# First attention: DVE's reciprocal and product of a chunk move behind the next chunk's first row maxima

## The chip, the cores and the metric

One core of a Trainium2 chip runs the whole program. The metric is the device time of one execution in microseconds (us). PE is TensorE, DVE is VectorE, ACT is ScalarE, POOL is GpSimd, SP is SyncE.

## The reference, cut to what matters

The program is an attention layer with clipped relative positions over 4096 tokens of width 256 (16 heads of 16), a layernorm, a two-layer local attention block and another layernorm. The change touches the first attention alone:

```python
qh, kh, vh = split(q @ in_proj_weight.T + in_proj_bias)      # 16 heads, d = 16
qh = qh / sqrt(d)
scores = einsum('bhid,bhjd->bhij', qh, kh)
bias_r = einsum('bhid,rd->bhir', qh, rel_pe)                 # 129 distances, clipped at 64
attn = softmax(scores + take_along_axis(bias_r, rel), axis=-1)
out = einsum('bhij,bhjd->bhid', attn, vh)
```

## The kernel before, in words

`attend` works through 128 chunks: 16 heads by 8 blocks of 512 queries, numbered n. Scores are exact to float32 by way of bfloat16 parts. For each chunk PE makes the scores twice. The first time, 32 products of 128 queries by 512 keys (`max_group`, L490) go one at a time into a bank of `shared_ps`, and DVE takes the maximum of every row of it (`bank_max`, L764 and 765). The second time, with keys in the rows (`score`, L516 and 519) and the row maxima subtracted in the same product, they go to `scores`, DVE adds the bias near the diagonal (`near_add`, L738 and 741), ACT takes the exponential of two tiles at a time (`exp_pair`, L639 to 642), and PE multiplies with the values (`pv_quad`, L531). PE puts four key tiles of one turn in four quarters of its array, so `out_ps` holds four partial sums. At the end of a chunk ACT copies `out_ps` to `out_copy` (L665), PE turns it with four transposes (`sum_quadrants`, L551), and DVE's `finish` adds the quarters (L773), takes the reciprocal of the softmax sum (L775) and multiplies (L777) into `attn`, which the trace calls tokens.

The engines are ordered by hand with semaphores. PE goes through a chunk in 8 turns: one value product, then four slots, each a max product for a later chunk (slot s of chunk n makes product 16 + s; from slot 16 on it is chunk n + 2's), and two or none of the score products of two turns further on. In turns 0 and 1 of chunks 0 to 118 half of the bias block nine further on comes last (`make_bias`, L542, 16 small products), which ACT moves to SBUF (L633). DVE goes through the same 32 slots: the maximum of each, with a near add or the finding and cutting of the row maxima (`find_max` L748, `cut_high` L755, `cut_low` L759) before or after some, and `finish` behind the last.

Three banks `shared_ps` go round among 36 uses in a fixed order, `SHARED_USES`: maxima 0 to 3, bias half 0, maxima 4 to 7, bias half 1, maxima 8 to 19, rows, maxima 20 to 31, sum. Before each use PE's `bank_free` (L460 to 475) waits for the reader of the use three places before. So slot 3 waits for the maximum of slot 0, the first bias half for the maximum of slot 1, slot 4 for that of slot 2, and slot 2 for the sum of the chunk before: by `normed`, which the product at L777 raises.

DVE, PE and ACT run pairs of chunks (even, odd) in loops; DVE's is `Fori(0, 63)` at L804 with the last two chunks written out behind it. I call the seam between an even and the next odd chunk inner, and the seam where a DVE loop goes round, from an odd to an even chunk, turning.

Of the kernel before, what the change touches and what calls it, by code (L numbers as in the profile page):

```python
# [19 lines left out]
ALU = mybir.AluOpType  # L20
AX = mybir.AxisListType
# [10 lines left out]
D = E // HEADS  # L32
# [13 lines left out]
VW = D + 1  # L46
# [187 lines left out]
def attend(nc, q_parts, k_parts, v_wide, rel_T, ident, attn):  # L234
# [10 lines left out]
    TOTAL = HEADS * CHUNKS  # L245
# [4 lines left out]
    with ExitStack() as ctx:  # L250
        sb = lambda name, shape, dt=F32: ctx.enter_context(nc.sbuf_tensor(name, shape, dt))
        ps = lambda name, shape, dt=F32: ctx.enter_context(nc.psum_tensor(name, shape, dt))
        sem = lambda name: ctx.enter_context(nc.semaphore(name))
# [22 lines left out]
        out_sum = sb("out_sum", [P, TPC, VW])  # L276
# [4 lines left out]
        inv_sum = sb("inv_sum", [P, TPC, 1])  # L281
# [31 lines left out]
        max_rows = sem("max_rows")  # L313
# [4 lines left out]
        pv_done = sem("pv_done")  # L318
        out_copied = sem("out_copied")
        out_summed = sem("out_summed")  # L320
        norm_step = sem("norm_step")
        normed = sem("normed")

        block = ctx.enter_context(nc.Block())
# [1 line left out]
        def place(n):  # L326

            return n // CHUNKS, n % CHUNKS
# [131 lines left out]
        def _(pe):  # L460
            def bank_free(n, bias, *use):

                at = SHARED_USES.index(use) - 3
                if not bias and at >= 0 and SHARED_USES[at][0] == "bias":
                    at -= 3
                m = n if at >= 0 else n - 1
                kind, i = SHARED_USES[at]
                if kind == "max":
                    pe.wait_ge(max_read, m * MAX_GROUPS + (MAX_GROUPS + LEAD + i + 3))
                elif kind == "bias":  # L470
                    pe.wait_ge(bias_read, (m + NEXT_GEN) * 2 + (i + 1))
                elif kind == "rows":
                    pe.wait_ge(max_placed, m + 2)
                else:
                    pe.wait_ge(normed, m + 2)

            def max_group(n, par, k, bank):

# [88 lines left out]
            def chunk(n, par, bias, ahead):  # L567


                for turn in range(QUADS):  # L570
                    pv_quad(n, par, turn)
                    for i in range(4):
                        slot = 4 * turn + i
                        if slot == ROWS_SLOT and ahead:
                            if ahead == 2:
                                bank_free(n, bias, "rows", 0)
                            max_to_rows(n + 1, 1 - par)
                        max_slot(n, par, bias, slot, ahead)
                        for c in SLOT_SCORES[i]:
                            if turn < QUADS - 2:  # L580
                                score(n, par, 4 * (turn + 2) + c)
                            elif ahead:
                                score(n + 1, 1 - par, 4 * (turn - QUADS + 2) + c)
                    if bias and turn < 2:
                        bank_free(n, bias, "bias", turn)
                        make_bias(n + NEXT_GEN, (par + NEXT_GEN) % 2, turn)
                if ahead == 2:
                    bank_free(n, bias, "sum", 0)
                else:
                    pe.wait_ge(max_placed, TOTAL)  # L590
                    pe.wait_ge(normed, n + 1)
                sum_quadrants(n, par)

            pe.wait_ge(consts_in, 32)
# [28 lines left out]
        @block.scalar  # L623
        def _(act):
            act.preload_act_table(ACT.Exp)
            act.sem_inc(exp_done, 2)
            for semaphore in (out_copied, normed, out_summed, max_rows):
                act.sem_inc(semaphore, 1)

            def keep_bias(block_no, half):  # L630
                h, b = place(block_no)
                act.wait_ge(bias_ready, block_no * 2 + half + 1)
                act.activation(near_bias[:, bass.ds(h % 2, 1), 1:TILES + 1, bass.ds(b * BLOCK_U + half * UG, UG)],  # L633
                               shared("bias", half).rearrange("p (a u j) -> p a j u", a=1, u=UG), ACT.Copy
                               ).then_inc(bias_read, 1)

            def exp_pair(n, s):
                if s in (0, 1, 2, PAIRS - 1):
                    act.wait_ge(near_added, n * 4 + {0: 1, 1: 2, 2: 3, PAIRS - 1: 4}[s])  # L639
                act.wait_ge(scores_ready, n * PAIRS + s + 1)  # L640
                act.wait_ge(pv_done, n * QUADS + s // 2 + 1)
                act.activation(probs[s % 4][:], scores[s % 2][:], ACT.Exp).then_inc(exp_done, 1)  # L642

            def place_max(n, par):
                act.wait_ge(max_rows, n + 2)
                act.activation(queries[par][ROWS:ROWS + MROWS, :], shared("rows", 0)[ROWS:ROWS + MROWS, :], ACT.Copy
                               ).then_inc(max_placed, 1)

            def chunk(n, par, bias, more):

                for s in range(4, PAIRS):
                    if s == PAIRS - 2 and more:
                        place_max(n + 1, 1 - par)
                    exp_pair(n, s)
                    if bias and s in (5, 7):
                        if s == 5:
                            act.wait_ge(window_ready, n + 1)
                        keep_bias(n + NEXT_GEN, s // 7)
                for s in range(4):
                    if more:  # L660
                        exp_pair(n + 1, s)
                    if s == 1:
                        act.wait_ge(pv_done, n * QUADS + QUADS + 2)
                        act.wait_ge(out_summed, n + 1)
                        act.activation(out_copy[:], out_ps[:], ACT.Copy).then_inc(out_copied, 1)  # L665

            act.wait_ge(cleared, 10)
            for e in range(NEXT_GEN):
                for half in range(2):
                    keep_bias(e, half)  # L670
            place_max(0, 0)
            for s in range(4):
                exp_pair(0, s)
            last_bias = (TOTAL - NEXT_GEN) // 2
            with act.Fori(0, last_bias) as m:
                for par in range(2):
                    chunk(m * 2 + par, par, True, True)
            chunk(2 * last_bias, 0, True, True)
            chunk(2 * last_bias + 1, 1, False, True)
            with act.Fori(last_bias + 1, TOTAL // 2 - 1) as m:  # L680
                for par in range(2):
                    chunk(m * 2 + par, par, False, True)
            chunk(TOTAL - 2, 0, False, True)
            chunk(TOTAL - 1, 1, False, False)

        @block.vector
        def _(dve):
# [77 lines left out]
                dve.tensor_reduce(group_max[par][:, k:k + 1], bank, AX.X, ALU.max  # L765
                                  ).then_inc(max_read, 1)

            def finish(n):
                h, c = place(n)
                dve.wait_ge(out_summed, n + 2)  # L770
                dve.wait_ge(normed, n + 1)
                quarters = shared("sum", 0).rearrange("p (t i e) -> p t e i", i=4, e=P // 4)
                dve.tensor_reduce(out_sum[:], quarters[:, :, 0:VW, :], AX.X, ALU.add).then_inc(norm_step, 1)  # L773
                dve.wait_ge(norm_step, n * 2 + 1)
                dve.reciprocal(inv_sum[:], out_sum[:, :, D:VW]).then_inc(norm_step, 1)  # L775
                dve.wait_ge(norm_step, n * 2 + 2)
                dve.tensor_tensor(attn[:, bass.ds(c * TPC, TPC), bass.ds(h * D, D)], out_sum[:, :, 0:D],  # L777
                                  inv_sum[:].to_broadcast([P, TPC, D]), ALU.mult).then_inc(normed, 1)

            def chunk(n, par, ahead):  # L780
                for slot in range(MAX_GROUPS):
                    k = LEAD + slot
                    if slot == NEAR_SLOTS[3]:
                        near_add(n, PAIRS - 1)
                    if ahead and slot in NEAR_SLOTS[:3]:
                        near_add(n + 1, NEAR_SLOTS.index(slot))
                    if k < MAX_GROUPS and ahead >= 1:
                        bank_max(n + 1, 1 - par, k, shared("max", slot))
                    if k >= MAX_GROUPS and ahead >= 2:
                        bank_max(n + 2, par, k - MAX_GROUPS, shared("max", slot))  # L790
                    if ahead >= 1 and MAX_GROUPS - 1 <= k <= MAX_GROUPS + 1:
                        (find_max, cut_high, cut_low)[k - MAX_GROUPS + 1](n + 1, 1 - par)
                finish(n)

            for k in range(MAX_GROUPS):
                bank_max(0, 0, k, shared_ps[k % 3][:])
# [4 lines left out]
                bank_max(1, 1, k, shared_ps[(MAX_GROUPS + k) % 3][:])  # L801
            for s in range(3):
                near_add(0, s)
            with dve.Fori(0, TOTAL // 2 - 1) as m:  # L804
                for par in range(2):
                    chunk(m * 2 + par, par, 2)
            chunk(TOTAL - 2, 0, 1)
            chunk(TOTAL - 1, 1, 0)


def layernorm_params(dve, pool, stats, mean, rstd, scratch, expo, step, first):
# [1025 lines left out]
```

## Time and profile before

| | us |
|---|---|
| median of 3 runs | 5559.55 |
| lowest, highest | 5557.49, 5559.81 |
| the profiled execution's own time | 5559.1 |
| its span | 5557.4 |
| PE busy in the span | 5118.3 (92%) |
| DVE busy | 4185.6 (75%) |
| ACT busy | 3111.0 (56%) |
| first and last quarter sum (L773) | 285.7, 3752.4 |

The quarter sum ends each of the 128 chunks, so the stage lasts some 3470 us of the span, and two neighbouring quarter sums mark one chunk's period. PE's matmuls are pipelined: a product of 512 columns is shown with 0.38 us, while the next starts 0.22 us after it. Busy shares therefore say less than the starts do.

### The profile page before, as it was taken

What the parts mean: (1) busy time and instruction counts of PE and PEld (TensorE: products, weight loads), DVE (VectorE), ACT (ScalarE), POOL (GpSimd) and SP (SyncE); (2) the same over time, 40 slices, a digit from 0 to 9 for tenths busy, and PEclk for the clock granted to TensorE, in tenths of its full rate; (3) what the DMA queues carried; (4) which work ended last, traced back from release to release, by engine and by line L of the source; (5) the groups of instructions that cost most, each with busy time, mean ns of one, the idle gap of its engine ahead of it and who ended that gap; (6) DMA issues with size and microseconds to landing.
All of it is one profiled execution on the core that took longest, in us unless ns stands there. A gap on an engine that the chain in (4) does not pass through costs nothing. (4 is left out here: it accounts for less than half of the span.)

```text
span 5557.4 us, 114988 instructions
## 1 busy us (share of the span) xinstructions
PE 5118.3 (92%) x33760; PEld 2655.6 (48%) x33760; DVE 4185.6 (75%) x8817; ACT 3111.0 (56%) x4539; POOL 997.1 (18%) x791
## 2 busy tenths in 40 slices
PE   7599999999999999999999999998599989899989
PEld 4233333333333333333333333334488867788866
DVE  6488888888888888888888888871477744677755
ACT  4266666666666666666666666670266532456521
POOL 0211111111111111111111111100233310233211
PEclk9599999999999999999999999995699999999999
DMA  6312212212122122121221211211200000000010
GB/s 203 76 49 55 54 48 54 52 52 54 49 55 54 48 54 54 49 54 48 54 54 48 55 48 48 52 40 33 95 1 0 0 17 0 17 0 0 1 38 23
DMA packets 199610, 248.32 MB, mean 45 GB/s; under 512 B 60575, under 2 KB 128485, under 8 KB 197733
## 3 DMA queue, kind: packets, MB, share of 16 engines
q1 hardware_dynamic: 194388, 226.76, 14.9%
q0 software_dynamic: 5136, 20.45, 1.9%
q8 instruction: 50, 0.82, 0.1%
q14 instruction: 36, 0.29, 0.0%
HBM read 210.72 MB, written 36.18 MB: 44 GB/s over the span
## 5 line engine op out<-in xcount | busy, mean ns | idle before, releaser
L765 DVE TENSOR_REDUCE group_max<-shared_ps 128x1 f32<-128x512 f32 x4096 | 2668.6, 686 | 536.6 <-PE shared_ps L490 430.6
L642 ACT ACTIVATE probs<-scores 128x1024 f32<-128x1024 f32 x2048 | 2012.0, 1021 | 995.7 <-PE scores L516 619.4
L490 PE MATMUL shared_ps<-keys,max_queries 96*128 96x512 bf16 x4096 | 1444.0, 385 | 10.8 <-issue 1.7
L516 PE MATMUL scores<-queries,keys 98*128 98x512 bf16 (+3 forms) x4096 | 1212.8, 370 | 92.6 <-ACT probs L642 91.5
L531 PE MATMUL out_ps<-probs,values 128*17 128x512 f32 x8192 | 1079.1, 599 | 0.4 <-ACT probs L642 0.4
L490 PEld LDWEIGHTS shared_ps<-keys,max_queries 96*128 96x128 bf16 x4096 | 395.2, 96 | 1149.2 <-DVE group_max L765 544.2
L231 POOL TENSOR_TENSOR near_window<-near_bias,one_f 128x1536 bf16<-128x1536 f32 x128 | 351.4, 2746 | 2909.1 <-DVE max_parts L759 2263.7
L516 PEld LDWEIGHTS scores<-queries,keys 98*128 98x128 bf16 x4096 | 359.0, 98 | 466.2 <-ACT probs L642 242.8
L542 PE MATMUL shared_ps<-block_q,block_table 96*128 96x32 bf16 x4096 | 271.6, 233 | 107.6 <-POOL block_q L427 80.7
L542 PEld LDWEIGHTS shared_ps<-block_q,block_table 96*128 96x128 bf16 x4096 | 231.3, 114 | 197.9 <-issue 148.6
L1191 POOL TENSOR_TENSOR norm<-norm,layer_expo 128x16 f32<-128x16 f32 x64 | 186.2, 2910 | 705.4 <-DVE norm L1577 705.4
L1449 ACT ACTIVATE sim_prob<-sim_prob,shift,norm 128x256 f32<-128x256 f32 x512 | 299.5, 588 | 10.0 <-DVE shift L1647 10.0
L531 PEld LDWEIGHTS out_ps<-probs,values 128*17 128x17 f32 x8192 | 136.1, 95 | 264.7 <-issue 191.4
L494 PE MATMUL shared_ps<-ident_b,near_window 128*128 128x128 bf16 x1536 | 255.4, 220 | 0.0
L633 ACT ACTIVATE near_bias<-shared_ps 128x512 f32 (+1 forms) x256 | 152.8, 597 | 179.5 <-PE shared_ps L542 179.4
L741 DVE TENSOR_TENSOR scores<-scores,near_bias 128x192 f32<-128x192 f32 (+2 forms) x768 | 234.2, 334 | 20.7 <-PE scores L516 16.5
L1297 PEld LDWEIGHTS bank<-v_kept,prob_T 128*128 128x128 f32 x2048 | 238.2, 192 | 7.5 <-issue 2.0
L1297 PE MATMUL bank<-v_kept,prob_T 128*128 128x64 f32 x2048 | 235.8, 274 | 1.2 <-DVE tokens L1609 1.2
L1429 ACT ACTIVATE squares<-bank 128x512 f32<-128x512 f32 x128 | 76.5, 598 | 262.5 <-PE bank L1250 262.5
L494 PEld LDWEIGHTS shared_ps<-ident_b,near_window 128*128 128x128 bf16 x1536 | 151.3, 99 | 123.3 <-issue 2.2
L1504 ACT ACTIVATE gate<-quad,b 128x512 f32<-128x512 f32 x96 | 66.1, 688 | 236.9 <-PE quad L1371 236.9
L1642 DVE CUSTOM_DVE_ANT_0 sim_prob<-quad,mask 128x256 f32<-128x256 f32 x512 | 181.9, 420 | 16.5 <-issue 13.3
(195 smaller groups left out, 5777.3 us busy)
## 6 DMA issues: line engine op xcount, KB each, us to landing
keys<-k_parts SPq DMA_DIRECT2D x384, 96.0 KB, 2.1
values<-v_wide SPq DMA_DIRECT2D x128, 272.0 KB, 2.7
keys<-k_parts SPq DMA_DIRECT2D x384, 64.0 KB, 2.0
keys<-k_parts SPq DMA_DIRECT2D x128, 132.0 KB, 2.4
k_parts<-part SPq DMA_DIRECT2D x96, 128.0 KB
queries<-q_parts SPq DMA_DIRECT2D x768, 16.0 KB, 1.7
max_queries<-q_parts SPq DMA_DIRECT2D x768, 16.0 KB, 1.7
keys<-k_parts SPq DMA_DIRECT2D x384, 32.0 KB, 1.9
```

The source lines that it names most:

```text
L231: return pool.tensor_tensor(out, in_, ones[:].to_broadcast(list(in_.shape)), ALU.mult)
L490: mm = pe.matmul(bank, max_queries[par][:, t * P:(t + 1) * P], keys[par][0:ROWS, (t + TPC * g) * P:(t + TPC * (g + 1)) * P], start=True, s ...
L494: mm = pe.matmul(bank[:, pos * P:(pos + 1) * P], near_window[par][:, slab, u:u + P], ident_b[:], start=False, stop=i == len(near) - 1)
L516: mm = pe.matmul(out[:, 0:cut], keys[par][:, c * P:(c + 1) * P], queries[par][:, 0:cut], start=True, stop=True)
L531: mm = pe.matmul(out_ps[32 * i:32 * i + VW, :], values[par][:, 4 * q + i, :], probs[(2 * q + i // 2) % 4][:, i % 2, :], start=q == 0, stop ...
L542: mm = pe.matmul(shared("bias", half)[:, i * TILES:(i + 1) * TILES], block_table[par][:, BLOCK_U - 1 - u:BLOCK_U - 1 - u + P], block_q[par ...
L642: act.activation(probs[s % 4][:], scores[s % 2][:], ACT.Exp).then_inc(exp_done, 1)
L741: ins = dve.tensor_tensor(part, part, near_bias[:, bass.ds(h % 2, 1), bass.ds(c * TPC + slab, 1), u:u + b - a], ALU.add)
L765: dve.tensor_reduce(group_max[par][:, k:k + 1], bank, AX.X, ALU.max).then_inc(max_read, 1)
L1191: pool.tensor_tensor(norm[par][:], norm[par][:], expo[:, 0:2 * LHEADS].rearrange("p (h a) -> p h a", a=1), ALU.pow).then_inc(S.norm_ready, 1)
L1297: mm = pe.matmul(o_ps[:, j * LD:(j + 1) * LD], prob_T[:, 2 * j + c, :], v[:, h * LD:(h + 1) * LD], start=c == 0, stop=c == 1)
L1449: ins = act.activation(prob[:, h, :], sim[:, h, :], ACT.Exp, bias=shift[:, head:head + 1], scale=norm[par][:, head, :], accum_out=total[:, ...
```

## The change

`finish` is cut in three. `add_quarters` (the sum) stays at the end of the chunk and raises `sum_read`; on this PE now waits for the sum bank, in place of `normed`. `invert` (the reciprocal) of chunk n stands in chunk n + 1 behind the maximum of slot 0, and `finish` (the product) behind the maximum of slot 1. The first two chunks are taken out of DVE's loop, which starts at 1, since chunk 0 has none before it; the last chunk's reciprocal and product stand behind the last chunk. The semaphore `norm_step` becomes `sum_read` and `inverted`.

```diff
--- before.py
+++ after.py
@@ -318,7 +318,8 @@
         pv_done = sem("pv_done")
         out_copied = sem("out_copied")
         out_summed = sem("out_summed")
-        norm_step = sem("norm_step")
+        sum_read = sem("sum_read")
+        inverted = sem("inverted")
         normed = sem("normed")
 
         block = ctx.enter_context(nc.Block())
@@ -472,7 +473,7 @@
                 elif kind == "rows":
                     pe.wait_ge(max_placed, m + 2)
                 else:
-                    pe.wait_ge(normed, m + 2)
+                    pe.wait_ge(sum_read, m + 2)
 
             def max_group(n, par, k, bank):
 
@@ -588,7 +589,7 @@
                     bank_free(n, bias, "sum", 0)
                 else:
                     pe.wait_ge(max_placed, TOTAL)
-                    pe.wait_ge(normed, n + 1)
+                    pe.wait_ge(sum_read, n + 1)
                 sum_quadrants(n, par)
 
             pe.wait_ge(consts_in, 32)
@@ -624,7 +625,7 @@
         def _(act):
             act.preload_act_table(ACT.Exp)
             act.sem_inc(exp_done, 2)
-            for semaphore in (out_copied, normed, out_summed, max_rows):
+            for semaphore in (out_copied, sum_read, normed, out_summed, max_rows):
                 act.sem_inc(semaphore, 1)
 
             def keep_bias(block_no, half):
@@ -765,21 +766,27 @@
                 dve.tensor_reduce(group_max[par][:, k:k + 1], bank, AX.X, ALU.max
                                   ).then_inc(max_read, 1)
 
-            def finish(n):
-                h, c = place(n)
+            def add_quarters(n):
                 dve.wait_ge(out_summed, n + 2)
                 dve.wait_ge(normed, n + 1)
                 quarters = shared("sum", 0).rearrange("p (t i e) -> p t e i", i=4, e=P // 4)
-                dve.tensor_reduce(out_sum[:], quarters[:, :, 0:VW, :], AX.X, ALU.add).then_inc(norm_step, 1)
-                dve.wait_ge(norm_step, n * 2 + 1)
-                dve.reciprocal(inv_sum[:], out_sum[:, :, D:VW]).then_inc(norm_step, 1)
-                dve.wait_ge(norm_step, n * 2 + 2)
+                dve.tensor_reduce(out_sum[:], quarters[:, :, 0:VW, :], AX.X, ALU.add).then_inc(sum_read, 1)
+
+            def invert(n):
+                dve.wait_ge(sum_read, n + 2)
+                dve.reciprocal(inv_sum[:], out_sum[:, :, D:VW]).then_inc(inverted, 1)
+
+            def finish(n):
+                h, c = place(n)
+                dve.wait_ge(inverted, n + 1)
                 dve.tensor_tensor(attn[:, bass.ds(c * TPC, TPC), bass.ds(h * D, D)], out_sum[:, :, 0:D],
                                   inv_sum[:].to_broadcast([P, TPC, D]), ALU.mult).then_inc(normed, 1)
 
-            def chunk(n, par, ahead):
+            def chunk(n, par, ahead, before):
                 for slot in range(MAX_GROUPS):
                     k = LEAD + slot
+                    if before and slot in (1, 2):
+                        (invert, finish)[slot - 1](n - 1)
                     if slot == NEAR_SLOTS[3]:
                         near_add(n, PAIRS - 1)
                     if ahead and slot in NEAR_SLOTS[:3]:
@@ -790,7 +797,7 @@
                         bank_max(n + 2, par, k - MAX_GROUPS, shared("max", slot))
                     if ahead >= 1 and MAX_GROUPS - 1 <= k <= MAX_GROUPS + 1:
                         (find_max, cut_high, cut_low)[k - MAX_GROUPS + 1](n + 1, 1 - par)
-                finish(n)
+                add_quarters(n)
 
             for k in range(MAX_GROUPS):
                 bank_max(0, 0, k, shared_ps[k % 3][:])
@@ -801,11 +808,15 @@
                 bank_max(1, 1, k, shared_ps[(MAX_GROUPS + k) % 3][:])
             for s in range(3):
                 near_add(0, s)
-            with dve.Fori(0, TOTAL // 2 - 1) as m:
+            for n in range(2):
+                chunk(n, n, 2, n > 0)
+            with dve.Fori(1, TOTAL // 2 - 1) as m:
                 for par in range(2):
-                    chunk(m * 2 + par, par, 2)
-            chunk(TOTAL - 2, 0, 1)
-            chunk(TOTAL - 1, 1, 0)
+                    chunk(m * 2 + par, par, 2, True)
+            chunk(TOTAL - 2, 0, 1, True)
+            chunk(TOTAL - 1, 1, 0, True)
+            invert(TOTAL - 1)
+            finish(TOTAL - 1)
 
 
 def layernorm_params(dve, pool, stats, mean, rstd, scratch, expo, step, first):
```

## Rows read from the trace of the kernel before

**Rows 1.** Busy us (instructions) of PE, PEld, DVE, ACT, POOL; PE clock; DMA; attention stage.

```profile
1500.00:2500.00 1000.00, 963.46 (x6653) 366.44 (x6651) 838.75 (x1593) 652.87 (x726) 163.08 (x138) 1.00 0.21 52
```

**Rows 2.** Waits of PE's weight loads, 286 to 3300 us: total, times, longest.

```profile
PEld shared_ps L490 <- DVE group_max L765: 448.8, 583, 0.9
```

**Rows 3.** Order of time, DVE, inner seam: start, duration, line, tiles, count.

```profile
1938.89 1.29 DVE L765 TENSOR_REDUCE group_max<-shared_ps 128x1 f32<-128x512 f32 x2 [0.18 <-PE shared_ps L490]
1940.09 0.43 DVE L773 TENSOR_REDUCE out_sum<-shared_ps 128x68 f32<-128x272 f32 x1
1940.56 0.18 DVE L775 RECIPROCAL inv_sum<-out_sum 128x4 f32<-128x4 f32 x1
1940.95 0.22 DVE L777 TENSOR_TENSOR tokens<-out_sum,inv_sum 128x64 f32 x1 [0.21 <-DVE inv_sum L775]
1941.09 0.68 DVE L765 TENSOR_REDUCE group_max<-shared_ps 128x1 f32<-128x512 f32 x1
...
1941.69 1.28 DVE L765 TENSOR_REDUCE group_max<-shared_ps 128x1 f32<-128x512 f32 x2
```

**Rows 4.** Order of time, PE, inner seam.

```profile
1938.47 0.60 PE L490 MATMUL shared_ps<-keys,max_queries 96*128 96x512 bf16 x2
...
1940.42 0.39 PE L490 MATMUL shared_ps<-keys,max_queries 96*128 96x512 bf16 x1
...
1941.08 0.38 PE L490 MATMUL shared_ps<-keys,max_queries 96*128 96x512 bf16 x1
...
1941.73 0.60 PE L490 MATMUL shared_ps<-keys,max_queries 96*128 96x512 bf16 x2
1942.50 0.50 PE L542 MATMUL shared_ps<-block_q,block_table 96*128 96x32 bf16 x6 [0.17 <-DVE group_max L765]
...
1944.49 0.39 PE L490 MATMUL shared_ps<-keys,max_queries 96*128 96x512 bf16 x1
```

**Rows 5.** Order of time, DVE, turning seam.

```profile
1967.49 0.43 DVE L773 TENSOR_REDUCE out_sum<-shared_ps 128x68 f32<-128x272 f32 x1
...
1968.35 0.23 DVE L777 TENSOR_TENSOR tokens<-out_sum,inv_sum 128x64 f32 x1 [0.21 <-DVE inv_sum L775]
...
1968.91 1.89 DVE L765 TENSOR_REDUCE group_max<-shared_ps 128x1 f32<-128x512 f32 x3 [0.33 <-PE shared_ps L490]
```

**Rows 6.** Order of time, PE, turning seam.

```profile
1967.82 0.39 PE L490 MATMUL shared_ps<-keys,max_queries 96*128 96x512 bf16 x1
...
1969.65 0.39 PE L490 MATMUL shared_ps<-keys,max_queries 96*128 96x512 bf16 x1
1970.33 0.90 PE L542 MATMUL shared_ps<-block_q,block_table 96*128 96x32 bf16 x13 [0.28 <-DVE group_max L765]
```

**Rows 7.** DVE's sequencer, ns: the loop's end, the product's registers.

```profile
L804 DVEq COMPARE_BRANCH  x63: 50/56/72, 314.5 to 3716.2; - x63
...
L777 DVEq FUSED_REGOPS  x126: 129/129/129, 286.4 to 3715.9; - x126
```

**Rows 8.** Order of time, DVE: the quarter sum one chunk later.

```profile
1995.22 0.43 DVE L773 TENSOR_REDUCE out_sum<-shared_ps 128x68 f32<-128x272 f32 x1
```

**Rows 9.** The same behind chunks without bias: inner, turning, inner seam.

```profile
3589.13 0.43 DVE L773 TENSOR_REDUCE out_sum<-shared_ps 128x68 f32<-128x272 f32 x1
...
3614.24 0.43 DVE L773 TENSOR_REDUCE out_sum<-shared_ps 128x68 f32<-128x272 f32 x1
...
3639.62 0.43 DVE L773 TENSOR_REDUCE out_sum<-shared_ps 128x68 f32<-128x272 f32 x1
```

**Rows 10.** Order of time, DVE: small operations between row maxima.

```profile
1955.34 0.16 DVE L755 TENSOR_SCALAR max_parts<-row_max 128x4 bf16<-128x4 f32 x1
1955.50 0.69 DVE L765 TENSOR_REDUCE group_max<-shared_ps 128x1 f32<-128x512 f32 x1
1956.11 0.15 DVE L759 SCALAR_TENSOR_TENSOR max_parts<-row_max,max_parts 128x4 bf16<-128x4 f32 x1
1956.26 1.29 DVE L765 TENSOR_REDUCE group_max<-shared_ps 128x1 f32<-128x512 f32 x2
```

## The prediction

> **What bounds the kernel now.** I read the table of engines over the attention stage first [rows 1]. From 1500 to 2500 us PE is busy for 963 us at full clock, DVE for 839, ACT for 653: the stage goes at PE's pace, with small holes, so a change on DVE is worth only what it takes out of PE's holes. Next the list of waits of PE and of its weight loads. At its head stand PE's max products, waiting for DVE's row maxima (L765) [rows 2]; the product of line 777, whose `normed` the sum bank waits for, is nowhere in it. Many of those idle times of PEld lie under running value products and cost nothing, so the seam between two chunks has to be read instruction by instruction.
>
> Two seams follow each other in time. DVE's loop holds two chunks. After the even one (the inner seam) DVE just goes on; after the odd one (the turning seam) it goes round its loop. Take DVE's quarter sum (L773) as zero: 1940.09 at the inner seam [rows 3], 1967.49 at the turning one [rows 5]. Up to there both are alike: reciprocal at +0.47, product at +0.86. Then the first row maximum starts at +1.00 (1941.09) at the inner seam, and at +1.42 (1968.91) at the turning seam, where the sequencer does the loop's end in between [rows 7]. On PE [rows 4, 6] slot 0's max product starts at +0.33 at both, slot 1's at +0.99. Slots 2 and 3 start at +1.64 and 0.22 us later at the inner seam (two products in 0.60 us, one alone 0.38); at the turning seam slot 3 slips to 1969.65, +2.16, just after the end of slot 0's maximum (1968.91 + 0.68). The half block of bias (L542) takes the bank of slot 1's maximum. That maximum starts 0.60 behind the first and ends at 1941.69 + 0.68 = 1942.37 (+2.28), and the bias starts at 1942.50 (+2.41), 0.13 us later; at the turning seam the same steps give 1968.91 + 0.60 + 0.68 = 1970.19, and the bias starts at 1970.33 (+2.84). PE could have begun it 0.22 us after slot 3, near +2.08. Each seam has a hole ahead of the bias: 0.33 us inner, 0.75 us turning.
>
> Does the hole reach the period? Between quarter sums lie 27.40 us behind an inner seam and 27.73 us behind a turning one [rows 3, 5, 8]: of 0.42 us more lateness 0.33 us arrives. Without bias halves (last chunks) it is 25.11 against 25.38 [rows 9].
>
> **The change part by part.**
>
> *The bank is given back by the sum instead of the product.* The bank comes free at +0.43 instead of +1.09 (0.86 + 0.23 us). Its next user is slot 2's product on PE at +1.64, with no idle time ahead of it [rows 4]. The cover is 0.55 us; worth 0.
>
> *Reciprocal and product leave the place ahead of the first maximum.* Slot 0's product starts at +0.33 and takes 0.39 [rows 3, 4, 6]; a maximum that waits for its product starts 0.04 after that model end (+0.33 + 0.39 + 0.04 = +0.76; the 0.04 as at 1938.47 + 0.38 against 1938.89 in [rows 3, 4]). The sum ends at +0.43, so DVE is free. The loop's end stood behind the product; now it stands behind the sum. From the product's start to the maximum's it took 0.56 us (1968.35 to 1968.91), so from the sum's start +0.56, before +0.76, even if the sequencer were no further ahead. Its 63 turns are thus covered by the wait for PE. Slot 0's maximum: +0.76 to +1.44 at both.
>
> *Reciprocal between the maxima of slots 0 and 1.* The trace has no reciprocal there, but it has two operations of the same size between maxima: `cut_high` and `cut_low`, 0.16 and 0.15 us, each with a wait on DVE's own semaphore, start 0.61 after a maximum's start and put the next one off by 0.16 [rows 10]. The bounds: 0.15 from below (`cut_low`) and, from above, all overlap lost, as rival 3 works out. I take the nearest, 0.16: reciprocal +1.36, maximum of slot 1 +1.52 (its product is there at 0.99 + 0.43 = +1.42), end +2.20, bias at +2.33. That is 0.08 earlier than now at the inner seam, 0.50 at the turning one (0.51 by rounding).
>
> *Product between slots 1 and 2.* It starts at +2.12, and its register work (0.13 us [rows 7]) fits under the running maximum. Maxima of slots 2 and 3 then start near +2.30 and +2.90, against +2.20 and +2.80 at the inner seam. Their banks are wanted by slots 4 and 5, and slot 4 runs at 1944.49, +4.40 [rows 4], 1.3 us after the maximum of slot 2 would end: worth 0. The four own-semaphore waits per chunk stay four. The two peeled chunks add code once, no work; the last chunk's reciprocal and product end the stage as before, worth 0.
>
> *What is late next.* Behind the bias PE runs the turns without a hole of this kind; the exponentials and near adds near the chunk's end follow PE's scores, and they moved with it at the turning seam. They keep 0.09 of 0.42.
>
> **Sum.** Chunks 1 to 118 make bias and lie behind a seam each: 59 of each kind. The 63 turns of DVE's loop leave four turning seams without bias [rows 7]. Turning: 0.33 (as measured between the kinds) + 0.08; inner: 0.08. 59 x 0.49 = 28.9 us. The four without bias: 25.38 - 25.11, 4 x 0.27 = 1.1 us. Together 30.0 us. The profiled execution took 5559.1 us (span 5557.4 and 1.7 around it); 5559.1 - 30.0 = 5529.1. The median of the runs is 0.45 above that execution: 5529.5 us. What a measurement can tell here is about 0.2%, 11.1 us.
>
> By the Trainium skill ("VectorE: DVE Perf Modes", The DRAIN you can't avoid) the next operation doesn't start until the pipe is empty, semaphores cost nothing extra, and what counts is the number of operations. By that alone the move would give PE the bank of slot 1 later, not earlier; rival 3 works out this mechanism from rows. The rows speak against it as an absolute rule: a maximum of 0.68 us is followed by the next 0.60 after its start [rows 3].
>
> **The rivals.**
> 1. *Only the loop's turn is cured.* The reciprocal costs 0.24 and not 0.16, so the inner seam gains nothing and the turning one exactly the measured 0.33: 59 x 0.33 + 1.1 = 20.6 us, 5539 us. For it: no reciprocal was seen in that place. Against: `cut_high` and `cut_low` [rows 10]. Chance 0.15.
> 2. *Everything passes.* The 0.09 us that got lost between lateness and period belong to the even chunk's code and not to a slack: 59 x (0.50 + 0.08) + 1.1 = 35.3 us, 5524 us. Chance 0.13.
> 3. *Slower: the reciprocal stands in front of the bias bank.* Place: between maxima 0 and 1 at all 118 seams. If each operation waits for the end of the one before and the sequencer prepares the next maximum's wait only then, the reciprocal starts at +1.48, ends +1.66, and slot 1's maximum comes 0.33 later (the idle time before a maximum at the turn [rows 5]): +1.99, end +2.67, bias +2.80. Inner +0.39, turning -0.03: 59 x 0.36 - 1.1 = 20 us slower, 5579 us; with the 0.21 us that the product waited behind the reciprocal [rows 3] instead, bias +2.68: 5567 us. It loses from a maximum of slot 1 later than about +1.77. For it: that 0.21 us. Against: that idle time was a true dependence plus register work, and slot 1 does not depend on the reciprocal. Chance 0.06, some of it within 0.2%.
> 4. *Nothing arrives.* PE is earlier at the bias and stands longer for the exponentials at the chunk's end, or the branch isn't hidden: within 3 us of 5559 us. Against: the two kinds of chunk show 0.33 of 0.42 arriving. Chance 0.08.
>
> The change can fail to do what it says only in its first half, and there I expect it: the earlier release is not what pays.
>
> **How the numbers follow.** Forecast 0.58. The range reaches from just past rival 2 (5524, with 4 us for what the later stages make of another start) to past rival 1 (5539, with 7 us for a mixture with rival 4): 5520 to 5546 us. Left out are rivals 3 and 4 and strays, under 2 in 10. Faster by over 0.2%: forecast, rivals 1 and 2, 0.86; within: rival 4 and a little of 3, 0.09; slower 0.05.
>
> **What would show it.** Right: the first maximum at +0.76 from the sum at both seams, reciprocal +1.36, slot 1's maximum +1.52, product +2.12, bias near +2.33 at both; slot 3 never at +2.16; periods near 27.3 us behind both seams. Wrong: a first maximum at the turn later than +0.8 (branch not hidden); over 0.2 us between reciprocal and slot 1's maximum (rivals 1, 3); bias at +2.33 but periods above 27.4 (rival 4); an idle time of PE on line 773 (the bank did matter).

## The result, and the profile after

| | before | after |
|---|---|---|
| median, us | 5559.68 (4 runs) | 5515.00 (4 runs) |
| span of the profiled execution | 5557.4 | 5512.2 |
| first to last quarter sum | 285.7 to 3752.4 | 287.4 to 3709.2 |
| period behind an inner seam | 27.40 | 27.21 |
| period behind a turning seam | 27.73 | 27.17 |

The ratio is 0.9919, with a 95% interval of 0.9902 to 0.9936: 44.7 us faster, where 30.0 were forecast, and below the range's lower end of 5520. Between the first and the last quarter sum lie 3421.8 us instead of 3466.7, so 44.9 us come from the attention stage. The first sum comes 1.7 us later and the rest of the program takes 2.0 us less. That rest has no edit in it; in the kernels below it took between 1803 and 1807 us, so I read nothing into it. In the experiments the kernel before ran again beside each: 5561.63 us (median of 18) with experiments 1 to 4, 5560.72 (one) with 5, 5560.80 (median of 7) with 6 and 7; their ratios are to these.

DVE at the inner seam after the change, in order of time (start, duration, line, tiles, count). It answers to [rows 3].

```profile
1919.45 0.43 DVE L773 TENSOR_REDUCE out_sum<-shared_ps 128x68 f32<-128x272 f32 x1
1920.20 0.69 DVE L766 TENSOR_REDUCE group_max<-shared_ps 128x1 f32<-128x512 f32 x1 [0.32 <-PE shared_ps L491]
1920.81 0.17 DVE L777 RECIPROCAL inv_sum<-out_sum 128x4 f32<-128x4 f32 x1
1920.90 0.66 DVE L766 TENSOR_REDUCE group_max<-shared_ps 128x1 f32<-128x512 f32 x1
1921.47 0.22 DVE L782 TENSOR_TENSOR tokens<-out_sum,inv_sum 128x64 f32 x1
```

PE at the same seam, answering to [rows 4].

```profile
1919.78 0.39 PE L491 MATMUL shared_ps<-keys,max_queries 96*128 96x512 bf16 x1
...
1920.44 0.38 PE L491 MATMUL shared_ps<-keys,max_queries 96*128 96x512 bf16 x1
...
1921.09 0.60 PE L491 MATMUL shared_ps<-keys,max_queries 96*128 96x512 bf16 x2
1921.69 1.07 PE L543 MATMUL shared_ps<-block_q,block_table 96*128 96x32 bf16 x16
```

With the sum as zero, the first maximum starts at +0.75, the reciprocal at +1.36, slot 1's maximum at +1.45, the product at +2.02, slots 2 and 3 of PE at +1.64 and 0.22 later, the bias half at +2.24. The turning seam, from the same two views, no longer differs ([rows 5, 6]; its sum is at 1946.66, and the bias half starts at +2.23):

```profile
1946.66 0.43 DVE L773 TENSOR_REDUCE out_sum<-shared_ps 128x68 f32<-128x272 f32 x1
1947.41 0.69 DVE L766 TENSOR_REDUCE group_max<-shared_ps 128x1 f32<-128x512 f32 x1 [0.32 <-PE shared_ps L491]
```

```profile
1948.30 0.60 PE L491 MATMUL shared_ps<-keys,max_queries 96*128 96x512 bf16 x2
1948.89 0.50 PE L543 MATMUL shared_ps<-block_q,block_table 96*128 96x32 bf16 x6
```

The next quarter sum is at 1973.83. So the bias half starts 0.17 us earlier at inner seams and 0.61 at turning ones, and the periods are 0.19 and 0.56 us shorter in these rows. Over the middle of the stage two chunks take 54.39 us instead of 55.13: 0.74 us a pair, 59 x 0.74 = 43.7 us.

### The profile page after: what moved, and what is told of

It is laid out like the page before. It is cut to its first block and busy times, and to the rows that moved or that the text cites. A ratio compares the mean times of both kernels' runs of the same rounds, so it can differ in the third digit from the quotient of the medians.

```text
span 5512.2 us, 114702 instructions
## 1 busy us (share of the span) xinstructions
PE 5105.0 (93%) x33760; PEld 2653.6 (48%) x33760; DVE 4166.2 (76%) x8817; ACT 3112.3 (56%) x4539; POOL 997.2 (18%) x791
```

## The experiments

Theory A throughout: at the seam PE waits with the bias half for slot 1's maximum, and whatever moves that maximum moves the period. The rivals stand with each run. Positions are counted from the quarter sum.

**1. The release alone.** The kernel before, with `sum_read` raised by the sum and PE waiting for it (the same wait stands a second time for the last chunks):

```diff
-                    pe.wait_ge(normed, m + 2)
+                    pe.wait_ge(sum_read, m + 2)
...
-                dve.tensor_reduce(out_sum[:], quarters[:, :, 0:VW, :], AX.X, ALU.add).then_inc(norm_step, 1)
+                dve.tensor_reduce(out_sum[:], quarters[:, :, 0:VW, :], AX.X, ALU.add).then_inc(sum_read, 1)
```

> The kernel before with one edit: PE's waits for the sum bank go to a semaphore that the quarter sum raises (sum_read) and no longer to the product's. Reciprocal and product stay where they were. Theory A (what counts is when the maximum of slot 1 ends, because the bias half waits for its bank): nothing moves, bias at +2.41 and +2.84 from the quarter sum, periods 27.4 and 27.7 us, 5560 us within 4. Rival B (the 15 us beyond the forecast come from the earlier release of the sum bank): periods shorter by 0.1 us, about 5545 us.

Measured: 5559.68 us, ratio to the kernel before 0.9996 (0.9986 to 1.0006). Bias at +2.41 and +2.84, periods 27.38 and 27.73. Alone, the first half of the change is worth nothing; rival B is out.

**2. The order alone.** The changed kernel, with PE waiting for the product again:

```diff
-                    pe.wait_ge(sum_read, m + 2)
+                    pe.wait_ge(normed, m + 2)
```

> The changed kernel with one edit: PE waits for the sum bank until the product has ended (normed), as before the change. Reciprocal and product stay behind the first maxima. Theory A: the product ends at +2.24, so slot 2's product on PE starts at +2.30 and not at +1.64, slot 3 at +2.52, the bias at +2.74: 0.33 us later than before the change at inner seams, 0.10 earlier at turning ones, and some 0.5 us per seam without bias: 59 x 0.23 + 4 = 18 us slower than before, about 5577 us. Rival C (the order alone brings the gain, the release is idle in every arrangement): 5515 us.

Measured: 5580.39 us, ratio 1.0030 (1.0018 to 1.0041): slower than the kernel before. PE in order of time at an inner seam (sum at 1948.82); the bracket is the idle time and who ended it:

```profile
1950.03 0.60 PE L517 MATMUL scores<-queries,keys 98*128 98x512 bf16 x2
1951.12 0.61 PE L491 MATMUL shared_ps<-keys,max_queries 96*128 96x512 bf16 x2 [0.49 <-DVE tokens L782]
1951.56 0.62 PE L543 MATMUL shared_ps<-block_q,block_table 96*128 96x32 bf16 x8
```

Slot 2 at +2.30 and bias at +2.74, as worked out. The release is idle while the product stands at +0.86 and is worth 65 us (5580 against 5515) once the product stands at +2.02. Rival C is out: the release alone is worth nothing, the order alone costs some 20 us, and together they bring 45.

**3. Only the loop's end out of the way.** The changed kernel with both operations at the start of the next chunk:

```diff
-                    if before and slot in (1, 2):
-                        (invert, finish)[slot - 1](n - 1)
+                    if before and slot == 0:
+                        invert(n - 1)
+                        finish(n - 1)
```

> The changed kernel with reciprocal and product moved to the very start of the next chunk, ahead of slot 0's maximum: the order of DVE's work is that of before, but the loop's end stands ahead of them. Theory A: reciprocal at +0.47, product at +0.86, first maximum at +1.00 at both seams, bias at +2.41 at both, periods 27.41 and 27.37: 59 x 0.35 + 1 = 22 us faster than before, 5538 us. So half of the change's 45 us is the loop's end. Rival D (the loop's end costs nothing of its own, it is only seen in the place where DVE stands idle): 5560 us.

Measured: 5545.9 us, ratio 0.9969 (0.9957 to 0.9982); 8 us above theory A's number. The inner seam is as expected (bias +2.41, period 27.39). At the turning seam DVE's rows, in order of time, show why:

```profile
1962.73 0.43 DVE L773 TENSOR_REDUCE out_sum<-shared_ps 128x68 f32<-128x272 f32 x1
1963.19 0.18 DVE L777 RECIPROCAL inv_sum<-out_sum 128x4 f32<-128x4 f32 x1
1963.76 0.22 DVE L782 TENSOR_TENSOR tokens<-out_sum,inv_sum 128x64 f32 x1 [0.38 <-DVE inv_sum L777]
1963.90 1.28 DVE L766 TENSOR_REDUCE group_max<-shared_ps 128x1 f32<-128x512 f32 x2
```

The product comes at +1.03 and not +0.86, behind an idle time of 0.38 us in place of the 0.21 of [rows 3]. The loop's end is hidden (no gap but this one), but the product's address now has the chunk before this turn's in it, and the view of its line shows 186 blocks of register work for 124 products, up to 206 ns long, where [rows 7] had one of 129 ns each:

```profile
L782 DVEq FUSED_REGOPS  x186: 62/129/206, 316.1 to 3678.9; - x186
```

So bias at +2.58 and period 27.52 at this seam: of the 0.42 us of the loop's end, 0.17 came back as register work. In the changed kernel the same work lies under slot 1's maximum and costs nothing. Expectation missed in this term, theory A kept; rival D is out by the 15 us gained.

**4. Half the turns.** The kernel before, DVE's loop with four chunks in its body:

```diff
-            with dve.Fori(0, TOTAL // 2 - 1) as m:
-                for par in range(2):
-                    chunk(m * 2 + par, par, 2)
+            with dve.Fori(0, TOTAL // 4 - 1) as m:
+                for step in range(4):
+                    chunk(m * 4 + step, step % 2, 2)
+            for step in range(2):
+                chunk(TOTAL - 4 + step, step, 2)
```

> The kernel before with DVE's loop of four chunks instead of two: 31 turns, not 63, nothing else moved. Theory A: 30 turning seams with bias and 2 without become inner ones, at 0.31 to 0.43 us and 0.27 us each: 10 to 13 us faster, 5547 to 5550 us; the periods behind the removed turns fall from 27.72 to 27.4 us and those behind the remaining ones stay. Rival D (the loop's end costs nothing): 5560 us.

Measured: 5729.84 us, ratio 1.0311 (1.0288 to 1.0334). Nobody expected that. DVE in order of time at a removed turn with the sum that follows it, and at a turn that is left with the sum that follows it:

```profile
2057.06 0.43 DVE L773 TENSOR_REDUCE out_sum<-shared_ps 128x68 f32<-128x272 f32 x1
...
2084.37 0.43 DVE L773 TENSOR_REDUCE out_sum<-shared_ps 128x68 f32<-128x272 f32 x1
...
2111.75 0.43 DVE L773 TENSOR_REDUCE out_sum<-shared_ps 128x68 f32<-128x272 f32 x1
...
2112.61 0.23 DVE L777 TENSOR_TENSOR tokens<-out_sum,inv_sum 128x64 f32 x1 [0.21 <-DVE inv_sum L775]
2115.82 0.69 DVE L765 TENSOR_REDUCE group_max<-shared_ps 128x1 f32<-128x512 f32 x1 [2.99 <-issue]
...
2144.43 0.43 DVE L773 TENSOR_REDUCE out_sum<-shared_ps 128x68 f32<-128x272 f32 x1
```

At the turn DVE stands 2.99 us for nothing that the profile names, and the period behind it is 32.68 us, 5.37 more than behind a removed turn (27.31). The idle time is only the first part of this. Slot 3's product waits for slot 0's maximum, so PE stands as well, and then its granted clock falls to half. PE in order of time, and the engines from 2116.37 to 2123.20 us (the last three numbers are PE's clock, the share of the DMA engines and GB/s):

```profile
2116.57 0.61 PE L490 MATMUL shared_ps<-keys,max_queries 96*128 96x512 bf16 x1 [2.80 <-DVE group_max L765]
```

```profile
2116.37:2123.20 6.83, 6.56 (x33) 2.36 (x34) 3.32 (x6) 1.96 (x3) 0.00 (x0) 0.50 0.00 0
```

PE stands for 2.80 us without a product. Near the end of that, at 2116.37, it is given half its clock, 1.2 GHz of 2.4, for 6.83 us, and the same product is shown with 0.61 us and not with 0.38. The first maximum comes 3.07 us later than behind a removed turn (+4.07, not +1.00); the other 2.3 us of the 5.37 I put down to this stretch at half clock. No run has the stall without the fall, so this split is not tested. Before it, and from 2123.20 to the chunk's end, the clock is full. So here the period grows by more than the lateness, the expectation that periods behind the remaining turns stay was missed, and theory A needs the condition that PE's clock stays where it was; over the attention stage of the kernel before and of the changed one the granted clock is 1.00.

The queues of the page have one line that changed much, the instruction queue q14, first of this kernel and then of the kernel before:

```profile
q14 instruction: 187, 1.53, 0.1%
```

```profile
q14 instruction: 36, 0.29, 0.0%
```

151 packets of instructions more for 31 turns, nearly five a turn, 1.2 MB in all. The Trainium skill ("Runtime: NRT & Kernel Launch", Instruction fetch mechanics) says that an engine holds a window of two blocks of instructions, that prefetch is sequential and that a taken branch out of the window has to fetch first; the packets and the 2.99 us agree with it, and the body of two chunks (0.33 us idle in [rows 5], few packets) seems to lie within it. I did not try a body of three. What this run was made for it shows all the same: behind the removed turn the period is 2084.37 - 2057.06 = 27.31 us against 27.73 [rows 5, 8]. All of the 0.42 us arrives. The expected gain of 10 to 13 us can't be seen in the time, since the turns that are left cost far more than it.

**5. A dose of lateness.** The changed kernel with two, then five more reciprocals behind the first:

```diff
+                for i in range(2):
+                    dve.reciprocal(spare[:, :, i:i + 1], out_sum[:, :, D:VW])
```

> The changed kernel with two more reciprocals of the same 128x4 into a spare tile right behind the first, between the maxima of slots 0 and 1. Theory A (a lateness of slot 1's maximum reaches the period in full): they put the maximum off by some 0.2 to 0.3 us in all, the bias by as much, and the periods behind both seams grow by the same amount, 118 times it: 5539 to 5551 us. Rival F (a quarter is absorbed at the chunk's end, as my sum had it): the periods grow by three quarters of the shift of the bias.

> The same with five more reciprocals. Theory A: the shift of the bias is two and a half times that with two more, and the periods follow it one to one: about 5575 to 5605 us. Rival F: three quarters of it.

DVE in order of time with two more (sum at 1928.32), and PE's bias half; the table below has medians over the stage's seams, so a single row can be 0.01 us off:

```profile
1929.68 0.17 DVE L778 RECIPROCAL inv_sum<-out_sum 128x4 f32<-128x4 f32 x1
1929.76 0.22 DVE L780 RECIPROCAL spare<-out_sum 128x4 f32<-128x4 f32 x2
1929.89 0.66 DVE L767 TENSOR_REDUCE group_max<-shared_ps 128x1 f32<-128x512 f32 x1
```

```profile
1930.68 0.50 PE L544 MATMUL shared_ps<-block_q,block_table 96*128 96x32 bf16 x6
```

| | bias half, inner and turning | period behind inner, turning | pair | one run (changed kernel: median of 4), us |
|---|---|---|---|---|
| changed kernel | +2.24, +2.24 | 27.21, 27.18 | 54.39 | 5515.0 |
| two more | +2.37, +2.37 | 27.34, 27.35 | 54.69 | 5533.6 |
| five more | +2.57, +2.56 | 27.54, 27.46 | 55.00 | 5553.7 |

The bias moves by 0.26 and 0.65 us a pair, the pair's period by 0.30 and 0.61: one to one within 0.04. Rival F (three quarters) would give 0.20 and 0.49. The other traces say the same of a pair, by medians: the change moves the bias by -0.77 us and the period by -0.74, experiment 2 by +0.24 and +0.27, experiment 3 by -0.25 and -0.22. The price was wrong again in the same direction: a reciprocal behind another puts the maximum off by 0.065 us, not by 0.1 or more, so both times stayed under theory A's ranges. By the time alone three quarters of the time that theory A adds (5533 to 5542 us with two more) would have fitted the first run; it is the periods, set against the bias in the same trace, that rule F out.

**6. Nothing between the first four maxima.** The reciprocal ahead of slot 4 and the product ahead of slot 5; and the reciprocal ahead of slot 0, the product ahead of slot 4:

```diff
-                    if before and slot in (1, 2):
+                    if before and slot in (4, 5):
```

> The changed kernel with the reciprocal ahead of slot 4's maximum and the product ahead of slot 5's, so that nothing stands between the first four maxima. Theory A: slot 1's maximum starts when its product is there, +1.41 instead of +1.45, bias at +2.21; periods shorter by 0.03 us, 3 us in all, about 5512 us. Rival E (the reciprocal between the maxima is what still holds the bias up): 0.09 us a seam, 5505 us.

```diff
+                    if before and slot in (0, 4):
```

> The changed kernel with the reciprocal ahead of slot 0's maximum, behind the loop's end, and the product ahead of slot 4's. Theory A: the reciprocal lies in the time in which DVE waits for slot 0's product (+0.43 to +0.75) and costs nothing: first maximum +0.75, second +1.41, bias +2.21, about 5512 us as with both later. Rival D' (a reciprocal ahead of the first maximum costs its 0.18 us or more): first maximum +0.9 or later, bias past +2.3, over 5522 us.

Measured, one run each: 5525.3 and 5515.6 us. In both, slot 1's maximum starts at +1.41 and the bias half at +2.23: without any reciprocal in the way it comes 0.01 us earlier. The reciprocal in its present place costs 0.04 us at the maximum and nearly nothing at PE, so rival E is out; and ahead of slot 0 it lies in the wait for PE, so D' is out. Theory A's gain of 3 us did not show either. With both later, periods are 0.07 us longer than the changed kernel's. The difference sits in turn 1: the second bias half waits for the bank of slot 5's maximum, and the product now stands ahead of that one. First DVE, then PE at that place (sum at 1923.03); in the changed kernel this half starts at +6.05, here at +6.13, and in the second order, with the product ahead of slot 4, at +6.04:

```profile
1928.29 0.21 DVE L782 TENSOR_TENSOR tokens<-out_sum,inv_sum 128x64 f32 x1
1928.42 1.28 DVE L766 TENSOR_REDUCE group_max<-shared_ps 128x1 f32<-128x512 f32 x2
```

```profile
1929.16 0.67 PE L543 MATMUL shared_ps<-block_q,block_table 96*128 96x32 bf16 x9
```

**7. The bias half one slot earlier.** If the wait of the bias half is the hole, another order on PE closes it. Made on the changed kernel and on the kernel before:

```diff
-        SHARED_USES = (max_uses[:4] + [("bias", 0)] + max_uses[4:8] + [("bias", 1)]
-                       + max_uses[8:ROWS_SLOT] + [("rows", 0)] + max_uses[ROWS_SLOT:] + [("sum", 0)])
+        SHARED_USES = (max_uses[:3] + [("bias", 0)] + max_uses[3:7] + [("bias", 1)]
+                       + max_uses[7:ROWS_SLOT] + [("rows", 0)] + max_uses[ROWS_SLOT:] + [("sum", 0)])
...
-                    if bias and turn < 2:
+                        if bias and turn < 2 and i == 2:
```

> The changed kernel with one edit on PE: in turns 0 and 1 of a chunk the half block of bias comes ahead of the fourth slot and not behind it, and has its place so in the order of the three banks. It then waits for the maximum of slot 0 (end +1.44) and not of slot 1 (+2.11). Theory A (the wait of the bias half for slot 1's bank was the last hole at the seam): bias at +1.87, slot 3 near +2.87, turn 1's value product 0.16 us earlier than at present at each of 118 seams; chunks without bias lose 0.25 us each, since slot 3 now waits for slot 1. 118 x 0.16 - 8 x 0.25 = 17 us under the changed kernel, about 5498 us. Rival G (the next limit, ACT's or DVE's work in the turn, stands right behind): 5512 us or more.

> The kernel before with that same edit on PE, and DVE's order left alone: sum, reciprocal and product ahead of the first maximum. Theory A: at inner seams slot 0's maximum ends at +1.68 and holds nothing up, so the bias starts at +1.87 and the seam is 0.33 us shorter; at turning seams it ends at +2.10, bias near +2.22, seam 0.39 shorter: 59 x 0.72 - 2 = 40 us, about 5519 us. The change's gain would then be had without it. Rival C (DVE must be rid of the two operations at that place): over 5545 us.

On the changed kernel: 5492.88 us, ratio to the kernel before 0.9884 (0.9867 to 0.9900), the fastest of all. PE in order of time at an inner seam (sum at 1904.35):

```profile
1905.99 0.38 PE L491 MATMUL shared_ps<-keys,max_queries 96*128 96x512 bf16 x1
1906.21 1.07 PE L543 MATMUL shared_ps<-block_q,block_table 96*128 96x32 bf16 x16
1907.11 0.40 PE L491 MATMUL shared_ps<-keys,max_queries 96*128 96x512 bf16 x1
1907.43 1.05 PE L532 MATMUL out_ps<-probs,values 128*17 128x512 f32 x8
```

The bias half follows slot 2 by 0.22 us, with no hole, and turn 1's value product comes at +3.08 instead of 1922.69 - 1919.45 = +3.24. Turn 1 gives a further 0.07 us that I had not counted; the periods are 26.98 and 26.94. The chunks without bias pay more than I had put down, 25.7 us instead of 25.1, 5 us in all.

On the kernel before: 5517.89 us, ratio 0.9927 (0.9910 to 0.9944), bias at +1.86 and +2.24, periods 27.00 and 27.27, as theory A has it. DVE's order is untouched there, so nearly the whole gain of the change is to be had without it. Rivals G and C are out. What the change buys is the bias half's wait, by whatever means.

## Why the prediction was wrong

**Right.** The mechanism and its places. PE's hole ahead of the bias half was the thing to read; the first maximum came at +0.75 (forecast +0.76), the reciprocal at +1.36 (as forecast), slot 3 no longer slipped, the loop's end disappeared under the wait for PE, and the release by itself was worth 0 (experiment 1).

**Wrong, first term: the reciprocal between two maxima, "I take the nearest, 0.16".** It puts slot 1's maximum off by 0.09 us, so this starts at +1.45, not +1.52; it is shown with 0.66 us where the forecast had 0.68, and the bias half starts at +2.24, not +2.33. The rows were misread. In [rows 10] `cut_high` is followed by a maximum 0.16 us later without idle time, and I took that for its price. PE in order of time in the kernel before, at those two maxima:

```profile
1955.18 0.28 PE L494 MATMUL shared_ps<-ident_b,near_window 128*128 128x128 bf16 x2
...
1955.95 0.28 PE L494 MATMUL shared_ps<-ident_b,near_window 128*128 128x128 bf16 x2
```

They end at 1955.46 and 1956.23, and the maxima start 0.04 and 0.03 us after, at 1955.50 and 1956.26. Each waited for its own near-window product; the small operation was hidden in that wait and set no lower bound. The maximum before these two, at 1954.73, starts as close behind the end of its near-window product (1954.42 + 0.28), and there the profile shows the wait for PE as idle time. The price of a small operation among others, 0.065 us in experiment 5, was in no row of before. Both bounds of this cost lay above the truth. At the bias half the miss is 0.09 us at 118 seams, 10.6 us.

**Wrong, second term: "They keep 0.09 of 0.42".** I compared a period behind an inner seam with one behind a turning seam, 27.40 and 27.73, and read the missing 0.09 us as a slack at the chunk's end. They belong to different chunks: the chunk behind an inner seam is odd, the one behind a turning seam even, and with the turn removed and nothing else the even one takes 27.31 (experiment 4). So 0.42 us arrive in full, as experiment 5 says at another place, and there was no slack. That is 0.09 us at 59 seams, 5.3 us. It was my rival 2, which I gave 0.13.

**Together.** 30.0 + 10.6 + 5.3 = 45.9 us, against 44.9 measured in the stage. Rival 2 alone gives 5524, inside the range; the reciprocal alone gives 5529.5 - 10.6 = 5519, at its very end; the two together 5514. The range let each vary while the other stood at its forecast, and the reciprocal could only get dearer in it, since its lower bound was false.

**A slip in rival 3.** Its second price, with bias at +2.68, should be 59 x (0.27 - 0.15) - 1.1 = 6 us slower, 5565 and not 5567. It decides nothing.

**A step that was right by luck.** "Worth 0" for the release was worked out with the product where it had been, at +0.86; the sum came out right in this term only because it took the release first. With the product at its new place, +2.02, the same subtraction gives slot 2 a wait of 0.66 us: the half that I called idle carries 65 us of difference (experiment 2). Rival 3 had each operation start behind the end of the one before, which here is +1.53 for slot 1's maximum; it started at +1.45. So the trace does not bear out, for independent operations, the rule that the prediction took from the Trainium skill ("VectorE: DVE Perf Modes", The DRAIN you can't avoid). The prediction gave that rule without its exception: the same section says that a next operation that is not held starts earlier, and with this the trace agrees.

**Open.** The two kinds of chunk don't lie a fixed time apart: 0.07 us in experiment 4 (27.38 against 27.31), 0.03 in the changed kernel (27.21 against 27.18), so that the 5.3 us hold for pairs and not for single periods. In experiment 4 both kinds stand alike up to turn 7's value product (+22.38, medians) and part behind it; what does it there was not looked for. Of the 0.04 us by which dose and period differ in experiment 5, of either sign, I only know that they are there. Why the body of four chunks has to be fetched at each turn and that of two has not was not tried by size.

## What to carry to other kernels

Before a row serves as the price of a small operation, look up what released the instruction behind it: with no idle time shown, it may still have waited for another engine, and the small operation was free. Compare periods only of chunks that run the same code, and vary two uncertain terms together when the range is made. When an order moves, work out every wait again with the new places: an early release that is idle in the old order can be what keeps the new one from losing. Before a long stall is priced by its idle time, look at PE's granted clock behind it.

## What the runs showed that I had not expected

A DVE loop whose body was doubled to four chunks stood for 2.99 us at the turn shown, with 151 instruction packets more in all; PE's clock then fell to half for 6.83 us, the period grew by 5.37, and the kernel lost 168 us (experiment 4). The loop of two chunks lost 0.42 us at a turn and left the clock alone. Small DVE operations of 128x4 follow each other every 0.065 us, though each is shown with 0.15 us. An address that reaches back over a loop's turn made the product's register work longer, 0.17 us more of idle time (experiment 3).
